# Second layer's projections of a four-layer graph network as three products of rounded halves and rests

## The chip, the cores and the metric

The kernel runs on one core of a Trainium2 chip. The metric is the device time of one execution in microseconds. The engines are TensorE (PE, matmuls), VectorE (DVE), ScalarE (ACT), GpSimd (POOL) and SyncE (SP, which here only issues transfers). Each engine works through its own instructions in the order in which they stand in the program, and semaphores order the engines against each other.

## What is computed

Four layers of a graph network, 1354 nodes with 256 features, one 1354x1354 adjacency matrix. Each layer is `x = x + layer(relu(layernorm(x)))`. The first layer (numbered 0 in the code) is an attention over all nodes. The change is in the second one (numbered 1):

```python
h  = relu(layernorm(x))
hW = h @ W_sa                                  # "h" items in the kernel
s_left, s_right = hW @ a_sa[0, :D], hW @ a_sa[0, D:]
e  = where(adj != 0, exp(-leaky_relu(s_left[:, None] + s_right[None, :], 0.01)), 0)
x_a = (e / (e.sum(1, keepdims=True) + 1e-5)) @ hW
x_b = adj @ (h @ W_gcnb) + b_gcnb              # "g" items in the kernel
attn_a = sigmoid(concat([adj @ h, h]) @ Wa.T + ba)
attn_b = sigmoid(concat([adj @ h, h]) @ Wb.T + bb)
x  = x + sigmoid(attn_a * x_a + attn_b * x_b)
```

The third and fourth layers are a neighbour mean with one projection and a masked attention.

## The kernel before, in words

The nodes are cut into NB = 11 blocks of up to 128 rows, and for the wide operands into NG = 3 groups of up to 512 columns. One n of NT = 33 "tiles" is a block of rows times a group. All data stays on the chip. Nearly every product of matrices is made exact enough in a cheap number format by splitting each operand into a rounded half and a rest (`hi` and `lo`, type float32r): ACT writes `hi`, DVE writes `lo = value - hi`, and PE adds three products, hi x hi, hi x lo, lo x hi (`products`, L333 to L337). The projections of the second layer are the exception: `project_full` (L1548 to L1551) multiplies plain float32 operands, two matmuls of 128x128 by 128x258 (or 260), each of which stands in the trace as two records.

The order of the work is written out by hand: each engine has a loop over steps `s`, and in step `s` it does a fixed list of things. Around the end of the first layer these are:

- PE, step s: `aggregate0(s-15)` (9 to 12 matmuls with the weights of tile s-15), and between them the second layer's first items: `turn(b, 1)`, which transposes normalised block b into PSUM bank 3 (one bank for all blocks, so `turn(b)` has to wait until block b-1 has been read out of it), `project_g(b)` and `project_h(b)`. Before: turn(0) in step 36, project_g(0) at the head of step 37, turn(1) to turn(3) at the ends of steps 37 to 39, project_g(1) to project_g(3) in steps 39 to 41, then turn(4) to turn(7) with the first project_h in steps 42 to 45. After the loop: project_h(4) to (7), and then the second layer's own aggregation `aggregate_b`, with turn(8) to turn(10) and the last projections between its tiles.
- ACT, step s: `exps(s-13)` (two exponentials), `z` (the normalised block), `h_full(b)` (L518: relu of the turned block into `h_mid`, plain float32), `g_hi` and `h1_hi` (rounded halves of the projections).
- DVE, step s: `weights_lo(s-14)` (L1004), `shift(s-12)` (L998), and in single steps more: `add_out(1)` in step 36 (L1012, L1016, four blocks of x), `stats` of three blocks in step 37 (L901), `stats`, four `aggr` and two small operations in step 38 (L901 to L911), `g_row_lo` in step 38 (L1028), `g_lo` from step 39 on (L1023). `weights_lo(n)` is what aggregate0(n) waits for before its last matmuls (L1642).
- POOL: `norm(1, 0)` and `norm(1, 1)` (L402, L409) turn the variances of the first eight blocks into scales; between them it has nothing to do.

The largest value of each column is found by `running` (L990), transposed by PE (`turn_max`, L1615), reduced on DVE (`top`, L958 to L966), spread again by PE (`spread_max`, L1624) and subtracted (`shift`). The last group's passes through this in steps 32 to 34.

`h_mid` lies in the memory of `mid_lo`, which the first layer's scores no longer need by then. The adjacency's rounded halves in the second layer (`adj_hi`, L684, on ACT; `adj_lo` on DVE, L1170, or POOL, L443) use the first columns of `mid_hi` and `mid_lo`.

Of the kernel before, what the change touches and what calls it, by code (L numbers as in the profile page):

```python
# [5 lines left out]
ALU = mybir.AluOpType  # L6
# [9 lines left out]
C = D // P  # L16
NB = -(-N // P)
# [21 lines left out]
def rows(b):  # L39
    return LAST if b == NB - 1 else P  # L40
# [64 lines left out]
def graph_layers_kernel(nc, x, adjT, wq, wk, wvT, wsa, wgcn, w2, w3, w3T, u3T, asa, cols, rws, eye, out):  # L105
    with ExitStack() as ctx:  # L106
# [3 lines left out]
        def sem(name):  # L110
            return ctx.enter_context(nc.semaphore(name))
# [64 lines left out]
        rb = sb("rb", [P, NB])  # L176

        hT0 = [t[:, 0:C * N].rearrange("p (c n) -> p c n", c=C) for t in (big_hi, big_lo)]
        hT3 = [t[:, :, :].rearrange("p b w -> p (b w)")[:, 0:C * N].rearrange("p (c n) -> p c n", c=C) for t in (v_hi, v_lo)]
        g = [t[:, :].rearrange("p (b w) -> p b w", w=W) for t in (big_hi, big_lo)]  # L180
        tT = [t[:, 0:C * N].rearrange("p (c n) -> p c n", c=C) for t in (mid_hi, mid_lo)]
# [74 lines left out]

        def h_block(b, layer):

            return [t[:, :, b * P:b * P + rows(b)] for t in (hT3 if layer == 3 else hT0)]

        ps = ctx.enter_context(nc.psum_tensor("ps", [P, 8, BANK], F32))
# [8 lines left out]
        def turns_before(layer):  # L270
            return NB * TURN_LAYERS.index(layer)
# [13 lines left out]
            sem(n) for n in ("col_set", "uw_set", "gram_set", "wlr_set", "wext_set"))  # L285
        whi, wlo = sems("whi", 7), sems("wlo", 7)
        st, mv, veps, rstd, ln = (sem(n) for n in ("st", "mv", "veps", "rstd", "ln"))
        zd, zt, hhi, hlo, h_set = (sem(n) for n in ("zd", "zt", "hhi", "hlo", "h_set"))
        x_add = sems("x_add", 4)
        t_mm, t_hi, t_lo = sems("t_mm", 2), sems("t_hi", 2), sems("t_lo", 2)  # L290
        v_mm, vhi, vlo = sems("v_mm", 2), sems("vhi", 2), sem("vlo")
# [22 lines left out]
        def wait(eng, s, value):  # L314

            if value > 0:
                eng.wait_ge(s, value)
# [7 lines left out]

        def h_done(eng, layer, count):

            if layer in (0, 3):
                wait(eng, hlo, (NB if layer else 0) + count)
            else:  # L330
                wait(eng, h_set, count)

        def products(eng, out_ap, lhs, rhs, first, last):  # L333

# [57 lines left out]
        def _(pool):  # L392
# [29 lines left out]
            pool.wait_ge(half_add, 1)  # L422
            for b in range(NB):
                add_bv(b)
            norm(1, 0)
            norm(1, 1)


# [73 lines left out]
        def _(act):  # L502
# [7 lines left out]
                act.activation(z_buf[:, b % 4, :], x_sb[:, b, :], ACT.Identity, bias=mr_all[:, b, 0:1],  # L510
                               scale=mr_all[:, b, 1:2]).then_inc(zd, 1)

            def h_full(b):

                act.wait_ge(zt, turns_before(1) + b + 1)
                if b == 0:
                    act.wait_ge(s_mm[0], NT)
                act.activation(h_mid[:, b, :, 0:rows(b)], turned(b, 1)[:, :, 0:rows(b)], ACT.Relu).then_inc(h_set, 1)  # L518

            def z2(b):  # L520

                act.wait_ge(ln, NG * 2 + b // PER + 1)
# [12 lines left out]
            def h_hi(b, layer):  # L535

                act.wait_ge(zt, turns_before(layer) + b + 1)
                act.activation(h_block(b, layer)[0], turned(b, layer)[:, :, 0:rows(b)], ACT.Relu).then_inc(hhi, 1)

            def t_hi_part(gi, a, parts=(0, 1)):  # L540
# [108 lines left out]
            for s in range(NB, NT + 13):  # L649
                if s >= 13:  # L650
                    exps(s - 13)
                if s == 11:
                    nonzero(1)
                    degree(1)
                elif 13 <= s < 31:
                    if s % 2:
                        nonzero((s - 13) // 2 + 2)
                    else:
                        degree((s - 13) // 2 + 2)
                if 33 <= s < 37:  # L660
                    z(s - 33, 1)
                if s == 35:
                    h_full(0)
                if 37 <= s < 40:
                    h_full(s - 36)
                if s == 37:
                    g_row_hi()
                if 38 <= s < 42:
                    g_hi(s - 38)
                if 39 <= s < 43:  # L670
                    z(s - 35, 1)
                if 42 <= s < 46:
                    h_full(s - 38)
                    h1_hi(s - 42)
                if 44 <= s < 46:
                    g_hi(s - 40)


            def adj_hi(n):

                wait(act, xb_mm, n - 2)
                if n == 0:
                    act.wait_ge(s_mm[0], NT)
                act.activation(adj_ring(at[0], n), adj_tile_b(n), ACT.Copy).then_inc(ahi, 1)  # L684

            def exp1(n):
# [51 lines left out]
            z(9, 1)  # L738
            z(10, 1)
            adj_hi(3)  # L740
            h_full(8)
            adj_hi(4)
            h_full(9)
            g_hi(8)
            h_full(10)
            exp1(0)
            g_hi(9)
            adj_hi(5)
# [137 lines left out]
        def _(dve):  # L886
# [26 lines left out]
            def h_lo(b, layer):  # L913

                hi, lo = h_block(b, layer)
                dve.wait_ge(hhi, (NB if layer else 0) + b + 1)
                dve.scalar_tensor_tensor(out=lo, in0=turned(b, layer)[:, :, 0:rows(b)], scalar=0.0, in1=f(hi), op0=ALU.max,
                                         op1=ALU.subtract).then_inc(hlo, 1)

# [194 lines left out]
            for s in range(NB, NT + LAG - 1):  # L1114
                if s == NB:
                    weights1_b()
                for gi in range(2):
                    if s == NB * gi + 12:
                        top(gi, 0, ALU.max)
                if s >= NT - 1:  # L1120
                    weights_lo(s - 14)
                if s == NT:
                    top(2, 0, ALU.max)
                for n in late_shifts(s):
                    shift(n, 0)
                if s < NT:
                    add(s)
                if s == 14:
                    weights_lo(0)
                if 13 <= s < NT - 1:  # L1130
                    shift(s - 13, 0)
                if 14 < s < NT - 1:
                    weights_lo(s - 14)
                for gi in range(2):
                    if s == NB * gi + 25:
                        add_out(gi)
                if s < NT:
                    running(s, 0, ALU.max)
                if s == 40:
                    dve.wait_ge(nz_sum, NB)  # L1140
                    dve.reciprocal(rdeg[:, :], deg[:, :]).then_inc(rdeg_set, 1)
                if 27 <= s < 31:
                    stats(s - 27, 1)
                if 27 < s <= 31:
                    aggr(s - 28, 1)
                if s == 37:
                    stats(4, 1)
                    stats(5, 1)
                    stats(6, 1)
                if s == 38:  # L1150
                    stats(7, 1)
                    for b in range(4, 8):
                        aggr(b, 1)
                if s == 38:
                    g_row_lo()
                if 39 <= s < 43:
                    g_lo(s - 39)
                if 43 <= s < 47:
                    h1_lo(s - 43)
                if 45 <= s < 47:  # L1160
                    g_lo(s - 41)
# [117 lines left out]
            adj_lo(2)  # L1279
            mask(1)  # L1280
            ramp(1)
            g_lo(8)
            adj_lo(4)
            g_lo(9)
            mask(2)
            ramp(2)
# [218 lines left out]
        def _(pe):  # L1505
# [39 lines left out]
                                   c == 0, c == C - 1)  # L1545
                return ins

            def project_full(out_ap, b, w, n):  # L1548

                for c in range(C):  # L1550
                    ins = pe.matmul(out_ap, h_mid[:, b, c, 0:rows(b)], w[:, c, 0:n], start=(c == 0), stop=(c == C - 1))  # L1551
                return ins

            def values(b, a):

                layer = 3 if a else 0
# [163 lines left out]
            def project_g(b):  # L1720

                h_done(pe, 1, b + 1)
                pe.wait_ge(wext_set, 2)
                pe.wait_ge(wg_in, 16)
                bank = item("g", b)
                project_full(ps[0:rows(b), bank, 0:W], b, raw_b, W).then_inc(g_mm, 1)

            def project_h(b):

                h_done(pe, 1, b + 1)  # L1730
                pe.wait_ge(wext_set, 1)
                pe.wait_ge(wsa_in, 16)
                bank = item("h", b)
                project_full(ps[0:rows(b), bank, 0:WA], b, raw_a, WA).then_inc(h_mm, 1)

            def lay_left(gi):

# [7 lines left out]
            for s in range(NB, NT + LAG):  # L1745
                if s < NT:
                    score(s, 0)
                if s == 36:
                    pe.wait_ge(s_sub[0], 2 * NB)
                    turn(0, 1)  # L1750
                if s == 37:
                    project_g(0)
                if s >= LAG:
                    aggregate0(s - LAG)
                for gi in range(NG):
                    if s == NB * gi + 11:
                        turn_max(gi, 0)
                    if s == NB * gi + 12:
                        spread_max(gi, 0)
                if 37 <= s < 40:  # L1760
                    turn(s - 36, 1)
                if 39 <= s < 42:
                    project_g(s - 38)
                if 42 <= s < 46:
                    turn(s - 38, 1)
                    project_h(s - 42)
                if 44 <= s < 48:
                    project_g(s - 40)
                if s == 46:
                    lay_left(0)  # L1770
# [261 lines left out]
```

## Time and profile before

| | |
|---|---|
| time before, median of 3 runs | 396.99 us (396.9 to 397.23) |
| profiled execution, its own time | 396.94 us |
| its span in the profile | 395.2 us |
| PE busy | 383.2 us (97%) |
| DVE busy | 336.9 us (85%) |
| ACT busy | 251.7 us (64%) |
| POOL busy | 121.9 us (31%) |
| mean granted clock of TensorE | 0.993 |

The second layer's first transposition starts at 103.8 us of the span, its last projection ends at about 151 us, and its aggregation runs up to about 240 us. A busy share of 97% on PE does not say that every us of PE work counts in full: in a stretch in which PE has no gap, time put on PE is time put on the kernel, and a stretch in which another engine is just ahead of PE has to be read separately. The PE records overlap in the trace, so the cost of a matmul is read from start to start, and not from its duration.

### The profile page before, as it was taken

The page shows a single profiled execution, that of the slowest core. Times are in us where ns is not written, and L with a number is a line of the kernel's source. Part 1 is how long each engine was busy: PE and PEld are TensorE (multiplying, and loading weights), DVE is VectorE, ACT ScalarE, POOL GpSimd, SP SyncE. Part 2 cuts the span into 40 slices and gives each one's busy share as a digit, 9 for nine tenths or more (in the row PEclk, how much of TensorE's full clock was granted, in tenths as well). Part 3 has the DMA queues.
Part 4 walks back from the last instruction along what each step waited for, and adds up shares of the span by engine and source line. Part 5 has one row for each costly group of instructions (what it writes and reads, how often), then busy time and mean ns, then how long its engine had stood idle before and what let it go on. Part 6 is the DMA issues. An engine that isn't in the chain of part 4 may idle for free. (4 is left out here: it accounts for less than half of the span.)

```text
span 395.2 us, 7759 instructions
## 1 busy us (share of the span) xinstructions
PE 383.2 (97%) x2647; PEld 354.4 (90%) x2647; DVE 336.9 (85%) x770; ACT 251.7 (64%) x531; POOL 121.9 (31%) x130
## 2 busy tenths in 40 slices
PE   8999999999999999999999999999999999989895
PEld 6888888999899899999999989998887898989894
DVE  5899899999984957999999989765887898799893
ACT  3553699888895658785787893245332576267772
POOL 1281000001010424223061011061010499379973
PEclk9999999999999999999999999999999999999988
DMA  7995000000000001000000000000000000010011
GB/s 233 375 380 189 0 2 1 2 0 2 0 2 0 2 1 55 2 2 0 3 2 0 3 0 2 2 1 0 2 2 0 2 1 2 0 55 1 2 54 37
DMA packets 10319, 13.99 MB, mean 35 GB/s; under 512 B 660, under 2 KB 7208, under 8 KB 10280
## 3 DMA queue, kind: packets, MB, share of 16 engines
q1 hardware_dynamic: 9736, 12.96, 9.6%
q10 hardware_dynamic: 544, 0.52, 0.4%
q8 instruction: 22, 0.36, 0.4%
q14 instruction: 17, 0.14, 0.1%
HBM read 12.10 MB, written 1.39 MB: 34 GB/s over the span
## 5 line engine op out<-in xcount | busy, mean ns | idle before, releaser
L1637 PE MATMUL ps<-v_hi,p_hi 128*128 128x258 f32 (+3 forms) x242 | 64.1, 295 | 0.3 <-DVE x_sb L1016 0.2
L402 POOL TENSOR_TENSOR mr_all<-mr_all,mhalf 128x4 f32<-128x4 f32 (+1 forms) x12 | 13.5, 1121 | 162.0 <-DVE mr_all L911 162.0
L1638 PE MATMUL ps<-v_lo,p_hi 128*128 128x258 f32 (+3 forms) x242 | 61.0, 282 | 0.0
L1637 PEld LDWEIGHTS ps<-v_hi,p_hi 128*128 128x128 f32 (+3 forms) x242 | 44.7, 185 | 2.1 <-issue 0.9
L1638 PEld LDWEIGHTS ps<-v_lo,p_hi 128*128 128x128 f32 (+3 forms) x242 | 44.8, 185 | 0.5
L1642 PE MATMUL ps<-v_hi,p_lo 128*128 128x258 f32 (+3 forms) x242 | 40.0, 283 | 1.1 <-DVE p_lo L1192 1.1
L998 DVE TENSOR_TENSOR s_sb<-s_sb,ps 128x512 f32<-128x512 f32 (+3 forms) x63 | 38.5, 612 | 1.3 <-PE ps L1624 1.2
L443 POOL TENSOR_TENSOR mid_lo<-adjT_sb,mid_hi 128x512 fp32r<-128x512 f32 (+2 forms) x16 | 22.5, 1406 | 48.5 <-ACT mid_hi L684 48.5
L1642 PEld LDWEIGHTS ps<-v_hi,p_lo 128*128 128x128 f32 (+3 forms) x242 | 32.5, 185 | 1.6 <-DVE p_lo L1192 1.6
L1928 PE MATMUL ps<-big_hi,p_lo 128*128 128x256 f32 (+3 forms) x121 | 32.2, 296 | 0.8 <-ACT p_lo L867 0.6
L1637 PE MATMUL ps<-big_hi,mid_hi 128*128 128x258 f32 (+3 forms) x121 | 31.8, 294 | 0.0
L1930 PE MATMUL ps<-big_lo,p_lo 128*128 128x256 f32 (+3 forms) x121 | 31.1, 287 | 0.0
L1638 PE MATMUL ps<-big_lo,mid_hi 128*128 128x258 f32 (+3 forms) x121 | 30.3, 282 | 0.0
L693 ACT ACTIVATE p_hi<-s_sb,minus_r 128x512 fp32r<-128x512 f32 (+3 forms) x33 | 22.1, 670 | 10.1 <-PE ps L1642 5.2
L1185 DVE SCALAR_TENSOR_TENSOR s_sb<-s_sb,sx 128x512 f32<-128x512 f32 (+3 forms) x33 | 26.0, 789 | 1.2
L990 DVE TENSOR_TENSOR m_sb<-m_sb,s_sb 128x512 f32<-128x512 f32 (+3 forms) x36 | 25.4, 704 | 0.7
L1928 PEld LDWEIGHTS ps<-big_hi,p_lo 128*128 128x128 f32 (+3 forms) x121 | 23.1, 191 | 2.5 <-ACT p_lo L867 2.1
L335 PE MATMUL ps<-mid_hi,v_hi 128*128 128x512 f32 (+3 forms) x66 | 25.2, 382 | 0.0
L335 PE MATMUL ps<-mid_hi,big_hi 128*128 128x512 f32 (+3 forms) x66 | 25.2, 381 | 0.0
L861 ACT ACTIVATE s_sb<-s_sb 128x512 f32<-128x512 f32 (+3 forms) x30 | 17.2, 574 | 11.4 <-DVE s_sb L998 11.3
L1426 DVE TENSOR_TENSOR w_lo<-ps,p_lo 128x512 fp32r<-128x512 f32 (+3 forms) x33 | 20.5, 620 | 4.7 <-ACT p_lo L867 3.2
L336 PE MATMUL ps<-mid_lo,big_hi 128*128 128x512 f32 (+3 forms) x66 | 24.3, 369 | 0.0
(249 smaller groups left out, 1217.9 us busy)
## 6 DMA issues: line engine op xcount, KB each, us to landing
adjT_sb<-in_adjT_dram SPq DMA_DIRECT2D x1, 2816.0 KB, 16.6
adjT_sb<-in_adjT_dram SPq DMA_DIRECT2D x3, 768.0 KB, 9.6
adjT_sb<-in_adjT_dram SPq DMA_DIRECT2D x1, 1815.0 KB, 21.5
out_dram<-x_sb SPq DMA_DIRECT2D x10, 128.0 KB
x_sb<-in_x_dram SPq DMA_DIRECT2D x2, 256.0 KB, 3.7
x_sb<-in_x_dram SPq DMA_DIRECT2D x1, 512.0 KB, 4.3
adjT_sb<-in_adjT_dram SPq DMA_DIRECT2D x1, 512.0 KB, 11.9
rows_sb<-in_rows_dram SPq DMA_DIRECT2D x1, 385.0 KB, 11.6
```

What stands on the lines that cost most here:

```text
L335: eng.matmul(out_ap, lhs[0], rhs[0], start=first, stop=False)
L336: eng.matmul(out_ap, lhs[0], rhs[1], start=False, stop=False)
L443: pool.tensor_tensor(adj_ring(at[1], n), adj_tile_b(n), f(adj_ring(at[0], n)), ALU.subtract).then_inc(alo_odd, 1)
L693: act.activation(ring(p_hi, n), sum1(n), ACT.Exp, bias=bias, scale=SLOPE - 1.0).then_inc(e_hi, 1)
L990: dve.tensor_tensor(m, m, mine(n), op).then_inc(s_max[a], 1)
L998: dve.tensor_tensor(mine(n), mine(n), ps[0:rows(j), bank, 0:CW[gi]], ALU.subtract).then_inc(s_sub[a], 1)
L1185: dve.scalar_tensor_tensor(out=sum1(n), in0=left[0:rows(j), gi, 0:CW[gi]], scalar=sx[0:rows(j), j, 0:1], in1=sum1(n), op0=ALU.add, op1=ALU ...
L1637: pe.matmul(out_ap, left_[0][0:k, n % RING, mine], right_[0][0:k, j, 0:cols_], start=(j == 0), stop=False)
L1638: pe.matmul(out_ap, left_[0][0:k, n % RING, mine], right_[1][0:k, j, 0:cols_], start=False, stop=False)
L1642: ins = pe.matmul(ps[0:rows(b), banks[b % PER], 0:cols_], left_[1][0:k, n % RING, mine], right_[0][0:k, j, 0:cols_], start=False, stop=(j ...
L1928: pe.matmul(sum3(b), p_lo[0:k, n % RING, mine], g[0][0:k, j, 0:D], start=(j == 0 and (gi == 2 or b % 2 == 0)), stop=False)
L1930: pe.matmul(sum3(b), p_lo[0:k, n % RING, mine], g[1][0:k, j, 0:D], start=False, stop=False)
```

## The change

Layer 1's turned blocks are now split as in the other layers: `h_hi` on ACT writes the half and a new `h_lo` on DVE the rest, 11 more DVE instructions. `project_full` goes; `project_g` and `project_h` call `project`, six float32r matmuls each. The weights are split too: ACT rounds `raw_b` in step 31 and `raw_a` in step 32, POOL subtracts both after `norm(1, 0)`. `project_g(0)` to `(3)` move from steps 37, 39, 40, 41 to steps 39 to 42, after the turn of their step. Since `h_done` now counts `hlo` in all layers, `turn(b, 1)` waits for `h_lo(b-1)` on DVE where it waited for `h_full(b-1)` on ACT. The waits of `adj_hi` change as well.

```diff
+        h1 = [t[:, :].rearrange("p (b c n) -> p b c n", b=NB, c=C) for t in (mid_lo, mid_hi)]
 ...
         def h_block(b, layer):
+            if layer == 1:
+                return [t[:, b, :, 0:rows(b)] for t in h1]
 ...
         def h_done(eng, layer, count):
-            if layer in (0, 3):
-                wait(eng, hlo, (NB if layer else 0) + count)
-            else:
-                wait(eng, h_set, count)
+            wait(eng, hlo, turns_before(layer) + count)
 ...   (POOL)
+            def weights_rest(k, lo, raw, hi):
+                pool.wait_ge(whi[k], 1)
+                pool.tensor_tensor(lo[:, :, :], raw[:, :, :], f(hi[:, :, :]), ALU.subtract).then_inc(wlo[k], 1)
             norm(1, 0)
+            weights_rest(4, wb_lo, raw_b, wb_hi)
+            weights_rest(3, wa_lo, raw_a, wa_hi)
             norm(1, 1)
 ...   (ACT; h_full goes, and each h_full(b) becomes h_hi(b, 1))
                 act.wait_ge(zt, turns_before(layer) + b + 1)
+                if layer == 1 and b == 0:
+                    act.wait_ge(s_mm[0], NT)
 ...
+                if s == 31:
+                    act.wait_ge(v_mm[0], NB)
+                    act.wait_ge(wg_in, 16)
+                    act.wait_ge(wext_set, 2)
+                    split(4, wb_hi[:, :, :], raw_b[:, :, :])
+                if s == 32:
+                    act.wait_ge(t_mm[0], 2 * NG)
+                    split(3, wa_hi[:, :, :], raw_a[:, :, :])
 ...
-                if 38 <= s < 42:
-                    g_hi(s - 38)
+                if 39 <= s < 43:
+                    g_hi(s - 39)
 ...
             def adj_hi(n):
-                if n == 0:
-                    act.wait_ge(s_mm[0], NT)
+                if n < RING:
+                    act.wait_ge(h_mm, 2 * n + 2)
 ...   (DVE)
+                if s == 36:
+                    h_lo(0, 1)
+                if 38 <= s < 41:
+                    h_lo(s - 37, 1)
                 if s == 38:
                     g_row_lo()
-                if 39 <= s < 43:
-                    g_lo(s - 39)
+                if 43 <= s < 47:
+                    h_lo(s - 39, 1)
+                if 40 <= s < 44:
+                    g_lo(s - 40)
 ...
             ramp(1)
+            h_lo(8, 1)
+            h_lo(9, 1)
             g_lo(8)
             adj_lo(4)
+            h_lo(10, 1)
             g_lo(9)
 ...   (PE)
-            def project_full(out_ap, b, w, n):
-                for c in range(C):
-                    ins = pe.matmul(out_ap, h_mid[:, b, c, 0:rows(b)], w[:, c, 0:n], start=(c == 0), stop=(c == C - 1))
-                return ins
 ...
-                pe.wait_ge(wext_set, 2)
-                pe.wait_ge(wg_in, 16)
+                pe.wait_ge(wlo[4], 1)
-                project_full(ps[0:rows(b), bank, 0:W], b, raw_b, W).then_inc(g_mm, 1)
+                project(ps[0:rows(b), bank, 0:W], b, 1, (wb_hi, wb_lo), W).then_inc(g_mm, 1)
 ...   (project_h likewise, with wlo[3], wa_hi, wa_lo)
-                if s == 37:
-                    project_g(0)
 ...
-                if 39 <= s < 42:
-                    project_g(s - 38)
+                if 39 <= s < 43:
+                    project_g(s - 39)
```

## Rows read from the trace of the kernel before

**Rows 1.** Busy time by stretch: us, then busy (instructions) of PE, PEld, DVE, ACT, POOL, clock
```profile
105.50:113.00 7.50, 7.50 (x53) 6.94 (x53) 7.37 (x25) 5.88 (x16) 1.44 (x2) 1.00 0.00 1
120.00:133.50 13.50, 13.50 (x84) 12.32 (x83) 7.38 (x22) 8.07 (x26) 0.78 (x3) 1.00 0.00 0
```
**Rows 2.** Timeline of PE, second layer's projections: start us, duration us, engine, line, operands
```profile
121.06 1.04 PE L1551 MATMUL ps<-raw_a,h_mid 128*128 128x260 f32 x4
121.94 1.03 PE L1551 MATMUL ps<-raw_b,h_mid 128*128 128x258 f32 x4
```
**Rows 3.** Timeline of PE: a first-layer projection in three products starts, the next work starts
```profile
29.79 0.28 PE L335 MATMUL ps<-wb_hi,big_hi 128*128 128x258 f32 x1
...
30.52 0.39 PE L335 MATMUL ps<-big_hi,wa_hi 128*128 128x512 f32 x1
```
**Rows 4.** Timeline of PE: project_g(0), then the starts of turn(1) and turn(2)
```profile
105.53 1.14 PE L1551 MATMUL ps<-raw_b,h_mid 128*128 128x258 f32 x4
...
107.84 0.38 PE L1512 MATMUL ps<-ident,z_buf 128*128 128x128 f32 x2
...
109.14 0.38 PE L1512 MATMUL ps<-ident,z_buf 128*128 128x128 f32 x2
```
**Rows 5.** Timeline of DVE, steps 37 to 39
```profile
107.43 0.49 DVE L1004 TENSOR_TENSOR p_lo<-s_sb,p_hi 128x330 fp32r<-128x330 f32 x1
...
111.06 0.42 DVE L1028 TENSOR_TENSOR big_lo<-rows_sb,big_hi 11x258 fp32r<-11x258 f32 x1
111.50 0.50 DVE L1004 TENSOR_TENSOR p_lo<-s_sb,p_hi 128x330 fp32r<-128x330 f32 x1
111.92 0.49 DVE L998 TENSOR_TENSOR s_sb<-s_sb,ps 128x330 f32<-128x330 f32 x1
```
**Rows 6.** DVE's groups by shape: the first layer's h_lo (count, busy us, mean ns)
```profile
L917 DVE SCALAR_TENSOR_TENSOR big_lo<-ps,big_hi 128x256 fp32r<-128x256 f32 x10 | 3.9, 413 | 0.0
```
**Rows 7.** Timeline of POOL: end of norm(1, 0), and a subtraction of 512 columns
```profile
98.96 0.20 POOL L409 TENSOR_TENSOR mr_all<-mr_all 128x4 f32<-128x4 f32 x1
...
139.04 1.09 POOL L443 TENSOR_TENSOR mid_lo<-adjT_sb,mid_hi 128x512 fp32r<-128x512 f32 x1 [1.26 <-ACT mid_hi L684]
```
**Rows 8.** Timeline of POOL (x_sb, 21.75 to 31.28) and of DVE's `running` beside and after it
```profile
21.75 9.53 POOL L415 TENSOR_TENSOR x_sb<-x_sb,rows_sb 128x256 f32<-128x256 f32 x11
...
29.42 1.25 DVE L990 TENSOR_TENSOR m_sb<-m_sb,s_sb 128x512 f32<-128x512 f32 x1
...
31.96 0.69 DVE L990 TENSOR_TENSOR m_sb<-m_sb,s_sb 128x512 f32<-128x512 f32 x1
```
**Rows 9.** Timeline of all engines, 98 to 102 us: the last column maxima, first layer
```profile
98.61 0.63 ACT L567 ACTIVATE p_hi<-s_sb 128x512 fp32r<-128x512 f32 x1 [1.42 <-DVE s_sb L998]
...
99.62 0.50 DVE L990 TENSOR_TENSOR m_sb<-m_sb,s_sb 74x330 f32<-74x330 f32 x1
...
100.17 0.55 PE L1615 MATMUL ps<-ident,m_sb 128*128 128x128 f32 x3 [0.61 <-DVE m_sb L990]
...
101.35 0.16 DVE L964 TENSOR_TENSOR mxr<-mxr,r_all 128x3 f32<-128x3 f32 x1
```
**Rows 10.** ACT and PE at turn(9): h_full(8), and the turn that waits for it
```profile
138.86 0.36 ACT L518 ACTIVATE h_mid<-ps 128x256 f32<-128x256 f32 x1
...
139.37 0.41 PE L1512 MATMUL ps<-ident,z_buf 128*128 128x128 f32 x2
```
**Rows 11.** PE's idle time in 226 to 229 us, clock unchanged
```profile
226.85 0.62 PE L1642 MATMUL ps<-v_hi,p_lo 128*128 128x258 f32 x3 [0.47 <-DVE p_lo L1192]
...
228.78 0.63 PE L1642 MATMUL ps<-v_hi,p_lo 128*128 128x258 f32 x3 [0.59 <-DVE p_lo L1192]
```
**Rows 12.** Busy time by stretch near the end: same columns as rows 1
```profile
371.00:372.00 1.00, 0.53 (x5) 0.32 (x3) 1.00 (x2) 0.77 (x2) 1.00 (x2) 1.00 0.00 0
...
373.00:374.00 1.00, 0.68 (x6) 0.55 (x5) 0.83 (x3) 0.88 (x3) 1.00 (x2) 1.00 0.00 0
...
375.70:379.10 3.40, 3.40 (x18) 3.40 (x18) 3.40 (x10) 2.79 (x7) 2.68 (x3) 0.50 0.06 22
```

More of the change, by code:

```diff
@@ L287, in graph_layers_kernel @@
         st, mv, veps, rstd, ln = (sem(n) for n in ("st", "mv", "veps", "rstd", "ln"))
-        zd, zt, hhi, hlo, h_set = (sem(n) for n in ("zd", "zt", "hhi", "hlo", "h_set"))
+        zd, zt, hhi, hlo = (sem(n) for n in ("zd", "zt", "hhi", "hlo"))
         x_add = sems("x_add", 4)
@@ L511, in z @@
                                scale=mr_all[:, b, 1:2]).then_inc(zd, 1)
-            def h_full(b):
-                act.wait_ge(zt, turns_before(1) + b + 1)
-                if b == 0:
-                    act.wait_ge(s_mm[0], NT)
-                act.activation(h_mid[:, b, :, 0:rows(b)], turned(b, 1)[:, :, 0:rows(b)], ACT.Relu).then_inc(h_set, 1)
             def z2(b):
@@ L662, in _ @@
                 if s == 35:
-                    h_full(0)
+                    h_hi(0, 1)
                 if 37 <= s < 40:
-                    h_full(s - 36)
+                    h_hi(s - 36, 1)
                 if s == 37:
                     g_row_hi()
-                if 38 <= s < 42:
-                    g_hi(s - 38)
+                if 39 <= s < 43:
+                    g_hi(s - 39)
                 if 39 <= s < 43:
@@ L672, in _ @@
                 if 42 <= s < 46:
-                    h_full(s - 38)
+                    h_hi(s - 38, 1)
                     h1_hi(s - 42)
@@ L681, in adj_hi @@
                 wait(act, xb_mm, n - 2)
-                if n == 0:
-                    act.wait_ge(s_mm[0], NT)
+                if n < RING:
+                    act.wait_ge(h_mm, 2 * n + 2)
                 act.activation(adj_ring(at[0], n), adj_tile_b(n), ACT.Copy).then_inc(ahi, 1)
@@ L740, in _ @@
             adj_hi(3)
-            h_full(8)
+            h_hi(8, 1)
             adj_hi(4)
-            h_full(9)
+            h_hi(9, 1)
             g_hi(8)
-            h_full(10)
+            h_hi(10, 1)
             exp1(0)
@@ L915, in h_lo @@
                 hi, lo = h_block(b, layer)
-                dve.wait_ge(hhi, (NB if layer else 0) + b + 1)
+                dve.wait_ge(hhi, turns_before(layer) + b + 1)
                 dve.scalar_tensor_tensor(out=lo, in0=turned(b, layer)[:, :, 0:rows(b)], scalar=0.0, in1=f(hi), op0=ALU.max,
@@ L1722, in project_g @@
                 h_done(pe, 1, b + 1)
-                pe.wait_ge(wext_set, 2)
-                pe.wait_ge(wg_in, 16)
+                pe.wait_ge(wlo[4], 1)
                 bank = item("g", b)
-                project_full(ps[0:rows(b), bank, 0:W], b, raw_b, W).then_inc(g_mm, 1)
+                project(ps[0:rows(b), bank, 0:W], b, 1, (wb_hi, wb_lo), W).then_inc(g_mm, 1)
             def project_h(b):
                 h_done(pe, 1, b + 1)
-                pe.wait_ge(wext_set, 1)
-                pe.wait_ge(wsa_in, 16)
+                pe.wait_ge(wlo[3], 1)
                 bank = item("h", b)
-                project_full(ps[0:rows(b), bank, 0:WA], b, raw_a, WA).then_inc(h_mm, 1)
+                project(ps[0:rows(b), bank, 0:WA], b, 1, (wa_hi, wa_lo), WA).then_inc(h_mm, 1)
             def lay_left(gi):
```

## The prediction

> **What bounds the kernel now.** I read first the busy time by stretch, around the end of the first layer. From 105.5 to 113 us PE is busy for all 7.50 of 7.50 us, and from 120 to 133.5 us again without a gap [rows 1]. So a us of PE work less is a us of kernel less there. The same rows carry the warning: in the first stretch DVE is busy for 7.37 of 7.50 us, in the second for 7.38 of 13.5. The change takes work from PE in both and puts work on DVE, and in the first DVE has no room. So I read next the timelines of PE and DVE over 97 to 120 us side by side, and then where POOL's new work would fall.
>
> **The gain on PE.** Two projections in a row start at 121.06 and 121.94 us [rows 2]: 0.88 us each. A first-layer projection of the same width in six float32r matmuls runs from 29.79 to 30.52 us: 0.73 us [rows 3]. There are 22 projections (11 g, 11 h): 22 x 0.15 = **3.3 us less**.
>
> **The new DVE work, and where it stands.** An h_lo takes 413 ns by its first-layer twin [rows 6]; back to back it adds about 0.34 us to the queue, since neighbours overlap by 0.08 (a weights_lo of 0.50 us is followed after 0.42 [rows 5]), and 0.41 until its result is there. From 120 us on DVE has room [rows 1], and nine of the eleven are hidden or nearly so. h_lo(0) and h_lo(1) are not, because of what `turn` now waits for. turn(2) needs h_lo(1). On DVE that stands in step 38, behind add_out(1), weights_lo(23), shift(25), three stats, weights_lo(24), shift(26), one stats, four aggr and two small ones, that is, exactly where g_row_lo stands before: 111.06 us [rows 5]. h_lo(0) ahead of it moves this by 0.34, and its own run takes 0.41: 111.81 us. Before, turn(2) started at 109.14 [rows 4]. So **turn(2) comes 2.7 us later**, whatever PE has saved by then, and everything that PE has behind it too. The wait falls in two parts: turn(1) already waits for h_lo(0), which stands behind add_out(1) (the next instruction starts at 107.43 [rows 5]) and ends at 107.84, while PE, without project_g(0) (0.88 us from 105.53 [rows 4]), reaches turn(1) at about 107.0.
>
> That 2.7 us does not yet hold project_g(0), which PE had done by then before and now has ahead of it: **+0.73 us**. Then turn(3) waits for h_lo(2), which follows g_row_lo, weights_lo(25) and shift(27) (0.44 + 0.42 + 0.42 [rows 5]) and takes 0.41: 1.7 us after h_lo(1), where PE needs 1.3 us from turn to turn [rows 4]: **+0.35** (0.4, less the last instruction's overlap). From turn(4) on, g_lo and h_lo keep up: between two turns PE has a tile and a projection of work, 1.1 + 0.73 us by [rows 3, 4], and in the stretch after, DVE was busy for only half of the time [rows 1].
>
> **The weights' split.** ACT idles for 1.42 us before exps(19) [rows 9]; the split of raw_b fits in, that of raw_a (about 0.6 us, as exps' own 512 columns take 0.63) delays exps(20), which has over 1 us in hand: nothing. The rests are on POOL, behind norm(1, 0), which ends at 99.16, each 516 or 520 columns, about 1.09 us [rows 7]: 99.2 to 100.3, and a second one behind it. At 99.62 DVE starts `running(32)`, whose result PE's turn_max is idle for (0.61 us, start 100.17 [rows 9]): the tightest place of this stretch. Both operands of `running` lie in SBUF, and the trace shows what that does beside POOL: during POOL's additions it takes 1.25 us, right after them 0.69 [rows 8]: 0.56 us more. If the second rest then lies over `top`'s two small additions (101.35 us [rows 9], also two SBUF operands), a further 0.0 to 1.1 us is at stake; I take that it starts after weights_lo(19), at 101.35, ends at 102.45 and holds the first of them until then. With the first delay of 0.6 to 0.7 the addition would be due at 102.0: 0.4 more. DVE's chain is then late by 1.1, and all of it comes back at turn(2), since DVE's queue has no gap of note on the way. Bounds: 0 (no hold, or POOL later than I think) and 2.2 (two full subtractions). I take **+1.1**.
> The Trainium skill's page SBUF — State Buffer, section "SBUF: two separate sides", says that a GpSimd instruction and a DVE instruction with two SBUF inputs exclude each other for a whole instruction, whichever started first. It speaks against this change. By it `running` would start only at POOL's end, 0.67 us late, where the row of 1.25 us gives 0.56; the sum would be 0.1 us higher.
>
> **Later waits.** turn(9) starts at 139.37, 0.15 us after h_full(8) ends (138.86 + 0.36) [rows 10]: it waited for it. Now h_lo(8) is in between, DVE being free: **+0.3**. And the four shorter project_h ahead of the second layer's first tile bring PE 0.6 us earlier to an adj_lo(0) that it already waited 0.2 us for, and DVE's queue ahead of that is shortened only in part: **+0.2**. adj_hi's new waits are for projections done long before: nothing.
>
> **The sum without the clock**: -3.3 + 2.7 + 0.73 + 0.35 + 1.1 + 0.3 + 0.2 - (project_g(0)'s 0.15 is in the 109.14 already, so only 21 savings count: +0.15) = **+2.2 us**.
>
> **The clock.** PE would stand still for about 1.2 us before turn(1) and 2.6 us before turn(2), with 1.2 us of work in between. The trace has two places with less. Idle times of 0.47 and 0.59 us within 2.4 us left the clock at 1.00 [rows 11]. Near the end, with PE busy 0.53 and 0.68 in two of three us (and eight matmuls of one column besides), it fell to 0.50, that is from 2.4 to 1.2 GHz, and stayed there from 375.7 to 379.1 us [rows 12]. Every us of PE work done so costs half a us. My idle time is above both, so I expect the fall, and a loss between 0 (it falls within the wait itself) and 2.6 us (it lasts twice as long, with the waits in it). I take **+1.5**, near the one stretch seen (half of 3.4, 1.7).
>
> Total: 396.94 + 2.2 + 1.5 = **400.6 us**. The profiled execution's 396.94 is 0.05 below the median, so nothing is added for that.
>
> **The rivals.**
> - *The waits, but no fall of the clock*, as at 226 us: +2.2, and with POOL's rests free as well +1.1: 398.0 to 399.2 us. For it: the rule of the fall is seen once only. Against: three times that idle time.
> - *The clock falls but POOL hinders nobody*: 396.94 + 1.1 + 1.5 = 399.5 us. For it: the first rest reaches the place only 0.4 us before `running` does (99.2 against 99.62), so a split or a norm that ends a little later puts it behind. Against: [rows 8], if it comes in time.
> - *More of everything*: both rests in DVE's way in full (2.2) and two stretches of slow clock: 396.94 + 3.3 + 2.6 = 402.8 us.
> - *The projections' gain comes through*: turn(2) finds h_lo(1) done. The place is DVE's step 38; it decides at whether h_lo(1) ends before PE reaches turn(2), at about 109.3. Then only the later waits remain: 396.94 - 3.3 + 0.5 = 394.1 us. Against it: the order of DVE's steps 36 to 38 has to be run through 1.8 us faster than it is now, with one instruction more. Only a misreading of the order would do it.
> - *Made good later*: PE waited 1.06 us for DVE at 226 to 229 [rows 11]; if DVE is not late with PE, up to 1.1 us comes back there; from the case without clock and POOL (+1.1) that ends at about 397.0 us, no change. Against: DVE's own start in the second layer hangs on PE's projections.
>
> **How the numbers follow.** Chances: the forecast 0.47, no fall of the clock 0.18, POOL hinders nobody 0.12, more of everything 0.11, made good 0.07, the gain comes through 0.05. Range: from 398.0 (the low end of the case without the clock) to 402.8. Slower by over 0.2% (0.8 us, about what a measurement of this kernel can tell from no change) are the first four, 0.88; within 0.2% is "made good", 0.07; faster is the last, 0.05.
>
> **What would show each step.** In the profile after: six matmuls per projection and starts 0.73 us apart; PE idle before turn(1) and before turn(2) at L1512, released by DVE's h_lo, 3 to 4 us in all; `running(32)` at about 1.2 us in place of 0.50 with POOL's subtraction beside it; granted clock 0.50 within some us behind turn(2). The prediction is wrong if turn(2) is not idle, which would say that I have DVE's order wrong; and too high by 1.5 if the clock stays at 1.00.

## The result and the profile after

The changed kernel takes 400.65 us (median of 4 runs, 399.49 to 400.89), against 396.99 before: ratio 1.0084, with an interval of 1.0070 to 1.0098. It is slower by 3.7 us. The profiled execution is the quickest of the four: 399.49 us, span 397.6, so 2.55 us over the profiled execution of before. That the other three are up to 1.4 us above it is part of the story.

The page's busy times, in the form of the table above:

```profile
span 397.6 us, 7847 instructions
...
PE 381.6 (96%) x2691; PEld 354.9 (89%) x2691; DVE 341.9 (86%) x781; ACT 253.3 (64%) x533; POOL 125.3 (32%) x132
```

PE is busy for 1.6 us less than before and the kernel is longer: the gain is there, and more than all of it went into waiting. Who PE waited for, in total, times, longest (us):

```profile
PE ps L1532 <- DVE mid_hi L928: 1.8, 3, 1.1
...
PE ps L1629 <- DVE m_sb L1001: 1.5, 2, 1.3
PE ps L1651 <- DVE x_sb L1027: 1.2, 2, 1.0
```

L1532 is `turn`, L928 `h_lo`, L1629 `turn_max` with `running` at L1001, and L1651 the first matmul of a tile, which waits for `add_out` at L1027. Before, the first wait was not there, the second was 0.8 us in all and the third 0.2 us. By stretch, in the columns of rows 1, the first line answers to its first line:

```profile
105.50:113.00 7.50, 5.35 (x31) 4.68 (x30) 7.25 (x25) 4.46 (x12) 0.77 (x1) 0.77 0.00 1
...
120.00:133.50 13.50, 13.50 (x116) 13.50 (x115) 8.58 (x22) 9.41 (x29) 0.47 (x2) 1.00 0.00 1
```

PE was busy for 7.50 of these 7.50 us; now 5.35, part of them at half clock, beside a DVE that is as full as before. In the second stretch it still has no gap: there the shorter projections pay nearly in full. The timelines of PE and DVE, with the idle time before an instruction and who ended it in brackets, answer to rows 4, 5 and 9:

```profile
98.92 1.30 POOL L429 TENSOR_TENSOR wb_lo<-raw_b,wb_hi 128x516 fp32r<-128x516 f32 x1
...
99.42 1.15 DVE L1001 TENSOR_TENSOR m_sb<-m_sb,s_sb 74x330 f32<-74x330 f32 x1
...
100.17 2.17 POOL L429 TENSOR_TENSOR wa_lo<-raw_a,wa_hi 128x520 fp32r<-128x520 f32 x1
...
100.63 0.55 PE L1629 MATMUL ps<-ident,m_sb 128*128 128x128 f32 x3 [1.27 <-DVE m_sb L1001]
...
101.81 0.56 DVE L975 TENSOR_TENSOR mxr<-mxr,r_all 128x3 f32<-128x3 f32 x1
...
107.28 0.36 PE L1651 MATMUL ps<-v_hi,p_hi 128*128 128x258 f32 x1 [1.02 <-DVE x_sb L1027]
...
108.92 0.63 PE L1532 MATMUL ps<-ident,z_buf 128*128 128x128 f32 x2
...
112.06 0.42 DVE L928 SCALAR_TENSOR_TENSOR mid_hi<-ps,mid_lo 128x256 fp32r<-128x256 f32 x1
...
112.62 0.41 PE L1532 MATMUL ps<-ident,z_buf 128*128 128x128 f32 x2 [1.13 <-DVE mid_hi L928]
...
114.35 0.41 PE L1532 MATMUL ps<-ident,z_buf 128*128 128x128 f32 x2 [0.24 <-DVE mid_hi L928]
```

The reader sees the chain of the prediction: beside POOL's first subtraction `running(32)` takes 1.15 us in place of 0.50, turn_max follows, beside the second one `top`'s first addition takes 0.56 in place of 0.16, and turn(2) starts at 112.62, when h_lo(1) (112.06 + 0.42) is done, 3.5 us later than in rows 4. At 107.28 stands a wait that the prediction did not have: aggregate0(22) waits for add_out(1). At turn(1) (108.92), where the prediction had a wait, there is none. And the projections, L335 to L337 in three products, follow each other 0.12 us apart from the second matmul on, as in rows 3.

### The profile page after: what moved, and what is told of

It reads as the page before. It is cut to its first block and busy times, and to the rows that moved or that the text cites. A ratio compares the mean times of both kernels' runs of the same rounds, so it can differ in the third digit from the quotient of the medians.

```text
span 397.6 us, 7847 instructions
## 1 busy us (share of the span) xinstructions
PE 381.6 (96%) x2691; PEld 354.9 (89%) x2691; DVE 341.9 (86%) x781; ACT 253.3 (64%) x533; POOL 125.3 (32%) x132
## 3 DMA queue, kind: packets, MB, share of 16 engines
HBM read 12.10 MB, written 1.39 MB: 34 GB/s over the span
## 5 line engine op out<-in xcount | busy, mean ns | idle before, releaser
L1651 PE MATMUL ps<-v_hi,p_hi 128*128 128x258 f32 (+3 forms) x242 | 63.3, 292 | 1.4 <-DVE x_sb L1027 1.2
L1651 PEld LDWEIGHTS ps<-v_hi,p_hi 128*128 128x128 f32 (+3 forms) x242 | 45.1, 186 | 3.0 <-ACT p_hi L570 1.2
L1651 PE MATMUL ps<-big_hi,mid_hi 128*128 128x258 f32 (+3 forms) x121 | 30.7, 285 | 0.0
L1001 DVE TENSOR_TENSOR m_sb<-m_sb,s_sb 128x512 f32<-128x512 f32 (+3 forms) x36 | 25.7, 715 | 0.7
L335 PE MATMUL ps<-mid_hi,v_hi 128*128 128x512 f32 (+3 forms) x66 | 25.2, 381 | 0.0
L335 PE MATMUL ps<-mid_hi,big_hi 128*128 128x512 f32 (+3 forms) x66 | 25.2, 381 | 0.0
```

The costliest lines, as they stand in the source:

```text
L335: eng.matmul(out_ap, lhs[0], rhs[0], start=first, stop=False)
L1001: dve.tensor_tensor(m, m, mine(n), op).then_inc(s_max[a], 1)
L1651: pe.matmul(out_ap, left_[0][0:k, n % RING, mine], right_[0][0:k, j, 0:cols_], start=(j == 0), stop=False)
```

## The experiments

### The changed kernel again, and its waits filled

The first question was the scatter, and whether the clock explains it. Beside a repetition, a kernel in which PE multiplies something during the waits:

```diff
+            def fill(count):
+                pe.wait_ge(s_add[0], NT)
+                pe.wait_ge(whi[4], 1)
+                for _ in range(count):
+                    pe.matmul(ps[:, 1, 0:W], wb_hi[:, 0, 0:P], wb_hi[:, 1, 0:W], start=True, stop=True)
 ...
+                if s == 37:
+                    fill(8)
                 if s >= LAG:
                     aggregate0(s - LAG)
+                if s == 38:
+                    fill(17)
```

> The changed kernel once more, unaltered, to have more executions of it beside those of the other kernels. Theory (the clock's fall costs an amount that depends on where it lies relative to the waits ahead of turn(1) and turn(2)): the times scatter by about 1.4 us (399.5 to 400.9 as so far) with an almost constant mean granted clock of 0.987 to 0.988. Rival (the 399.49 of the profiled execution was an outlier of another kind): all within 0.4 us of 400.7.

> The changed kernel with PE's waits filled: 8 more float32r matmuls of 258 columns (0.12 us each, 0.96 us) ahead of aggregate0(22), where PE idled 1.02 us, and 17 more (2.0 us) between aggregate0(23) and turn(2); they write a PSUM bank that nobody reads before it is written anew. Clock theory: PE no longer looks idle, the granted clock stays at 1.00 over 105 to 118 us, turn(2) starts when h_lo(1) is done as before (112.6), and the time is 399.2 to 399.6 in every execution, some 1.2 us under the changed kernel's median and with less scatter. Rival (the clock costs nothing here, or falls for another reason): 400.6 or, if the filling itself is in the way, up to 401.5.

Measured: the repetition 400.6 us (399.78 to 401.22, ratio 1.0082, 1.0069 to 1.0095), the filled one 399.84 (399.49 to 400.31, ratio 1.0068, 1.0056 to 1.0080). The repetition's profiled execution is its slowest, 401.22, and shows what the first one hid. First the repetition, then the filled kernel (busy time by stretch, same columns):

```profile
108.00:113.00 5.00, 2.65 (x21) 2.11 (x19) 4.93 (x19) 2.31 (x6) 0.41 (x1) 1.00 0.00 2
...
114.50:117.70 3.20, 3.18 (x16) 3.02 (x16) 1.97 (x6) 1.43 (x5) 0.00 (x0) 0.53 0.02 5
```

```profile
108.00:113.00 5.00, 4.67 (x38) 4.17 (x37) 4.93 (x19) 2.10 (x6) 0.62 (x1) 1.00 0.01 2
114.50:117.70 3.20, 3.20 (x27) 3.20 (x28) 2.10 (x6) 2.24 (x6) 0.00 (x0) 1.00 0.02 5
```

In the repetition PE idles for 2.35 of 5 us at full clock, and behind that runs from 114.5 to 117.7 at about half, 16 matmuls where the filled kernel does 27. turn(2) starts 13.2 us behind `running(32)` in both (112.99 and 112.77), so the filling neither helped nor hindered the wait itself. From turn(2) to the wait for adj_lo(0) in the second layer's first tile the repetition then takes 26.4 us and the filled kernel 25.1: the slow stretch costs 1.3 of the 1.55 us between the two executions. In the first profile the fall lay elsewhere:

```profile
108.10:111.45 3.35, 3.35 (x16) 2.98 (x16) 3.35 (x10) 1.86 (x5) 0.00 (x0) 0.52 0.01 2
```

There the slow stretch came before turn(2)'s wait: aggregate0(23) took longer, and PE then idled 1.13 us instead of 2.35. turn(2) is again 13.2 us behind `running(32)`, and 25.1 us follow to adj_lo(0): the slow clock was spent in time that PE had to wait anyway, which is 1.3 of the 1.7 us by which that execution is faster than the repetition's. So the fall is real, and in the one trace with filled waits it is absent; it costs 0 or 1.3 us according to where it lies. Between the two medians lie 0.8 us, though two of the repetition's five executions (399.78, 399.89) are among the filled kernel's times. What decides where it falls is not shown: idle times of 1.27 and 1.02 us were followed by it in the first profile, and of 1.27 and 1.06 us were not in the repetition. The expected median of 399.2 to 399.6 was a little missed (399.84), and so was "less scatter": 0.8 us remain, at mean granted clocks of 0.986 to 0.998; the kernel before scatters by 0.9 us at 0.985 to 0.998.

### POOL's subtractions: at another time, alone, and in the gaps

Three kernels. The first moves them to an earlier place (halves in steps 13 and 15, subtractions ahead of norm(1, 0)); the second adds nothing but the split to the kernel before; the third starts them right behind two `running`s:

```diff
+            pool.wait_ge(s_max[0], 27)
+            weights_rest(3, wa_lo, raw_a, wa_hi)
+            pool.wait_ge(s_max[0], 28)
+            weights_rest(4, wb_lo, raw_b, wb_hi)
             norm(1, 0)
-            weights_rest(4, wb_lo, raw_b, wb_hi)
-            weights_rest(3, wa_lo, raw_a, wa_hi)
 ...   (ACT: the halves in steps 23 and 25 instead of 31 and 32)
```

> The changed kernel with the weights split in steps 13 and 15 instead of 31 and 32, and POOL's two subtractions ahead of norm(1, 0), so that they lie near 45 us instead of 98.9 to 102.3 us. Theory (POOL's subtractions hold back running(32) and top's small addition, and DVE brings that lateness to turn(2)): running(32) takes 0.50 us again instead of 1.15, PE's idle time at L1629 is 0.6 instead of 1.27 us, h_lo(1) and turn(2) come 1.0 to 1.1 us earlier, and the median is 399.4 to 399.8. Rival 1 (the lateness is absorbed): unchanged, 400.4 to 400.8. Rival 2 (the subtractions hurt as much at 45 us): unchanged too, but with a running of about 1.2 us near 45 us and a PE wait there.

> The kernel before with only the weights' split added (ACT in steps 31 and 32, POOL behind norm(1, 0)); nothing reads the halves, the projections are plain float32. Theory (running(32) is held back by 0.65 us and top's first addition by 0.4, and PE waits for both): 0.8 us more than before, 397.7 to 398.0, with running(32) at 1.15 us. Rival (without the turn's wait for DVE, DVE's lateness does not reach PE beyond the 0.65 us at turn_max, or is made good): 397.0 to 397.5.

> The changed kernel with the weights' halves written in steps 23 and 25 and POOL's two subtractions started right behind running(29) and running(30), where DVE's next instructions (stats, add, shift, 1.3 us) have at most one operand in SBUF. Theory (a subtraction of 1.1 us on POOL costs only if a DVE instruction with two SBUF operands falls on it): no weights_lo or running in 90 to 100 us is longer than 0.70 us, PE's wait at L1629 is 0.6 us, turn(2) is 1.0 us earlier than in the changed kernel, median 399.4 to 399.8. Rival (any place in the first layer costs the same, since DVE or ACT is the bound there throughout, as with the subtractions at 52 and 58 us): 400.5 to 400.9.

Measured: earlier place 400.85 us (399.64 to 401.27), as rival 2 had it, though with the places near 52 and 58 us. The split alone 398.2 (398.03 to 398.44, ratio 1.0027, 1.0017 to 1.0037; the kernel before, measured beside it, 397.19): **+1.0 us**, a little over the 0.8 expected. In the gaps 399.69 (398.93 to 399.87, ratio 1.0061, 1.0048 to 1.0073): **0.9 us less** than the repetition (0.8 by the ratios), as expected. What the first did, on POOL, DVE and PE:

```profile
52.54 1.32 POOL L429 TENSOR_TENSOR wb_lo<-raw_b,wb_hi 128x516 fp32r<-128x516 f32 x1 [21.64 <-ACT wb_hi L512]
...
53.18 1.23 DVE L1001 TENSOR_TENSOR m_sb<-m_sb,s_sb 128x512 f32<-128x512 f32 x1
...
56.26 0.75 PE L1656 MATMUL ps<-v_hi,p_lo 128*128 128x258 f32 x4 [0.34 <-DVE p_lo L1015]
```

The same hold, 0.55 us, only in another step, and PE waits for DVE there instead; the second subtraction, at 57.70 us, holds a weights_lo for 0.95 us, and PE waits another 0.26. At neither place did DVE have slack. The kernel with the subtractions in the gaps has them beside instructions with at most one operand in SBUF:

```profile
93.96 0.49 DVE L1005 TENSOR_TENSOR m_sb<-m_sb,s_sb 128x330 f32<-128x330 f32 x1
...
94.53 1.31 POOL L429 TENSOR_TENSOR wb_lo<-raw_b,wb_hi 128x516 fp32r<-128x516 f32 x1 [1.09 <-DVE m_sb L1005]
...
95.17 0.68 DVE L1013 TENSOR_TENSOR s_sb<-s_sb,ps 128x512 f32<-128x512 f32 x1
...
96.37 0.50 DVE L1005 TENSOR_TENSOR m_sb<-m_sb,s_sb 128x330 f32<-128x330 f32 x1
```

No `running` is held, and turn_max starts at 100.02 us (before: 100.17). So it is neither POOL's work nor ACT's that costs, but the overlap with a DVE instruction that reads both operands from SBUF. The Trainium skill, SBUF — State Buffer, section "SBUF: two separate sides", says that these two exclude each other for a whole instruction. The trace agrees in kind, and in size about: in the changed kernel POOL's first subtraction starts at 98.92 and is recorded up to 100.22; `running(32)`, issued at 99.42, ends at 100.57, so that its own 0.50 us begin at 100.07. It is 0.65 us late, where the recorded end would give 0.80; the 0.67 and 0.56 of the prediction were for slightly other start times, so this case does not choose between them.

### project_g(0) one step later, alone

The kernel before, with project_g(0) to (3), g_hi and g_lo in the steps of the change and nothing else.

> The kernel before with only the order changed: project_g(0) to (3), g_hi and g_lo one step later, plain float32 projections, turn waits for ACT as before. Theory (project_g(0) covered the time until add_out(1) has emptied a bank for aggregate0(22)): PE idles 0.7 to 0.9 us ahead of aggregate0(22) and the kernel takes 0.8 us more, 397.7 to 397.9. Rival (PE works ahead and the wait is only moved): 396.9 to 397.2.

Measured: 398.08 us (397.85 to 398.33, ratio 1.0023, 1.0013 to 1.0033): **+0.9 us**, as the theory had it. On PE:

```profile
106.44 0.36 PE L1637 MATMUL ps<-v_hi,p_hi 128*128 128x258 f32 x1 [0.89 <-DVE x_sb L1016]
```

In the kernel before, project_g(0) (0.88 us) was what PE did while DVE emptied a PSUM bank for the last group of tiles. Taking it away left the hole.

### The turn's wait for DVE, alone

The kernel before with the 11 `h_lo` on DVE at the places of the change; they write a rest that nobody multiplies.

```diff
                 if turned_before(b, layer):
-                    h_done(pe, layer, turned_before(b, layer))
+                    wait(pe, hlo, turns_before(layer) + turned_before(b, layer))
 ...   (DVE)
+                if s == 36:
+                    h_lo(0, 1)
+                if 38 <= s < 41:
+                    h_lo(s - 37, 1)
 ...   (and 43 <= s < 47, and h_lo(8) to (10), as in the change)
```

> The kernel before (plain float32 projections, project_g(0) at the head of step 37, weights not split) with only DVE's part of the change: an h_lo per block at the places of the change, which writes a rest that nobody multiplies, and turn(b, 1) waiting for it. Theory (turn(2) waits for h_lo(1), which stands where g_row_lo stood): turn(2) at 111.8 to 112.0 instead of 109.14, turn(3) up to 0.35 us later still, turn(9) 0.3 us later: 3.2 to 3.4 us more than before without a fall of the clock (400.2 to 400.5), up to 402 with it. Rival (part of this wait is made good later, as PE waits for DVE near 226 us anyway): 398.5 to 399.5.

Measured: 401.9 us (401.14 to 402.5), ratio 1.0110 (1.0094 to 1.0125), the kernel before beside it 397.25: **+4.65 us**, the largest part by far.

```profile
107.94 0.41 PE L1527 MATMUL ps<-ident,z_buf 128*128 128x128 f32 x2
111.77 0.41 PE L1527 MATMUL ps<-ident,z_buf 128*128 128x128 f32 x2 [2.36 <-DVE mid_hi L918]
```

turn(2) at 111.77 in place of 109.14 is 2.6 us, where rows 4 to 6 gave 2.7. By the same trace turn(3) adds 0.45 us and turn(9) 0.45, and the clock, which fell behind this wait too (mean 0.87 over 105 to 118 us), 1.4. This trace is of the slowest of the four executions (402.5 us), so the 4.65 us probably hold less of the clock's price than that.

### h_lo(1) ahead, and a new order

Is it h_lo(1) alone? The changed kernel with h_lo(1) right behind weights_lo(24):

> The changed kernel with h_lo(1) on DVE directly behind weights_lo(24) instead of behind shift(26), a stats, four aggr and two small ones. Theory (turn(2) waits for h_lo(1) and for nothing else): turn(2) 1.2 to 1.3 us earlier relative to the start of add_out(1), PE's wait there nearly gone at half clock, the rest of the step as before, median 399.2 to 399.8. Rival (exps or weights_lo of the next steps become late instead, since shift(26) comes 0.34 us later): 400.2 to 400.8.

Measured: 399.79 us (399.7 to 402.58, ratio 1.0079, 1.0056 to 1.0102). The median would suit the theory, but the timeline does not:

```profile
112.03 0.41 PE L1534 MATMUL ps<-ident,z_buf 128*128 128x128 f32 x2 [1.47 <-DVE mid_hi L928]
...
114.65 0.66 PE L1534 MATMUL ps<-ident,z_buf 128*128 128x128 f32 x2 [1.14 <-DVE mid_hi L928]
```

turn(2) comes 1.0 us earlier than in the repetition, and turn(3) at 114.65 where it was at 114.72: h_lo(2), which still stood behind DVE's variances, took over. Nothing of note was won up to turn(3); with a scatter from 399.7 to 402.6 the median says little. The queue had to be reordered as a whole: h_lo(0) ahead of add_out(1), h_lo(1) and (2) behind their step's shift, stats and aggr spread over three steps, project_g(0) back at the head of step 37, together with POOL's subtractions in the gaps.

```diff
+                if s == 36:
+                    h_lo(0, 1)
+                if s in (37, 38):
+                    h_lo(s - 36, 1)
                 for gi in range(2):
                     if s == NB * gi + 25:
                         add_out(gi)
 ...
-                if s == 37:
-                    stats(4, 1)
-                    stats(5, 1)
-                    stats(6, 1)
-                if s == 38:
-                    stats(7, 1)
+                if s in (37, 38):
+                    stats(s - 33, 1)
+                if s == 39:
+                    stats(6, 1)
+                    stats(7, 1)
                     for b in range(4, 8):
                         aggr(b, 1)
```

> The changed kernel with the subtractions as in the one behind running(29) and (30), and a new order: h_lo(0) ahead of add_out(1), h_lo(1) and h_lo(2) right behind shift(25) and shift(26), the four stats and aggr spread over steps 37 to 39, g_row in steps 41 and 42, z(4) to z(7) one step later, project_g(0) back at the head of step 37 and (1) to (3) in 39 to 41. Theory (the three products' gain of 3.2 us is real and only DVE's order around steps 36 to 38 ate it): PE waits 0.3 to 0.6 us for h_lo(0), under 0.5 us in all at turn(1) to turn(3), the clock stays up, and the median is 393.9 to 395.0, faster than both. Rival (DVE's extra 3.8 us of h_lo has to be paid in this stretch whatever the order): 396.5 to 398.

Measured: 396.2 us (396.07 to 396.91), ratio 0.9981 (0.9972 to 0.9990): faster than both, and below the rival's 396.5 to 398, but 1.2 us short of what was expected. Two waits remained in its trace:

```profile
105.79 0.39 PE L335 MATMUL ps<-wb_hi,mid_lo 128*128 128x258 f32 x1 [0.49 <-DVE mid_hi L932]
...
119.33 0.41 PE L1537 MATMUL ps<-ident,z_buf 128*128 128x128 f32 x2 [0.67 <-DVE mid_hi L932]
```

A further order takes h_hi ahead of z on ACT, g_row later, h_lo(0) ahead of shift(24), h_hi(8) ahead of adj_hi(3):

> The kernel with the subtractions behind running(29) and (30) and the new order, further: h_lo(0) ahead of shift(24), h_hi(4) to (7) ahead of z on ACT, g_row in step 45 on ACT and 46 on DVE, h_hi(8) ahead of adj_hi(3). Theory (what that kernel still lost were PE's waits of 0.49 us ahead of project_g(0), 0.67 us at turn(5), where h_hi(4) stood behind z and g_row on ACT, and 0.45 us at turn(9)): project_g(0)'s wait 0.1 us, none at turn(5), 0.1 to 0.3 at turn(9), and 1.0 to 1.3 us less than its 396.2: 394.9 to 395.2. Rival (the next thing in the queue takes over): 395.6 to 396.2.

Measured: **395.65 us** (395.33 to 396.17), ratio 0.9961 (0.9948 to 0.9973): 1.6 us faster than the kernel before. It is 0.55 us less than 396.2 (0.8 by the ratios), not the 1.0 to 1.3 expected: this is the rival's range. The waits at turn(5) and turn(9) are gone; that ahead of project_g(0) stayed, as h_lo(0) now waits for ACT's h_hi(0):

```profile
105.47 0.42 DVE L933 SCALAR_TENSOR_TENSOR mid_hi<-ps,mid_lo 128x256 fp32r<-128x256 f32 x1 [0.25 <-ACT mid_lo L543]
...
105.95 0.39 PE L335 MATMUL ps<-wb_hi,mid_lo 128*128 128x258 f32 x1 [0.42 <-DVE mid_hi L933]
```

### The gain of the three products, in that order

The same kernel, with the two projections as plain float32 matmuls on the rounded half.

> The kernel of better order with the projections back to two plain float32 matmuls each, on the rounded half of the block and the unsplit weights; the rests are still made and waited for, but not multiplied, so the projections leave out the rests' part. Theory (a plain projection takes 0.88 us of PE, three products 0.73, and PE is the bound wherever the 22 stand): 3.0 to 3.3 us more than the kernel of better order. Rival (part of the shorter projections is only waited away): 1.5 to 2.5 us more.

Measured: 398.86 us (397.7 to 399.24), 3.2 us more than the kernel of better order. But 1.05 us of three of these five executions lie outside the profiled span: time and span differ there by 2.94 to 2.96 us, and by 1.7 to 2.1 us in all other executions of these kernels; what it is, is not shown. By the spans alone, median 396.2 against 393.8, the plain projections cost **2.4 us more**, which is the rival's range of 1.5 to 2.5. The traces say the same: from project_g(0) to the waits at 225.13 (better order) and 227.47 us (plain) the difference grows by 2.5 us. Of the 22 x 0.15 = 3.3 us the first is lost whole. First the tile behind project_g(0) in the kernel of better order (project_g(0) at 105.95, above), then project_g(0) and that tile with plain projections:

```profile
107.06 0.36 PE L1657 MATMUL ps<-v_hi,p_hi 128*128 128x258 f32 x1
```

```profile
105.79 1.14 PE L1577 MATMUL ps<-raw_b,mid_lo 128*128 128x258 f32 x4 [0.41 <-DVE mid_hi L933]
106.90 0.36 PE L1663 MATMUL ps<-v_hi,p_hi 128*128 128x258 f32 x1
```

Both take 1.11 us from project_g(0) to the start of aggregate0(22), which is the tile that waits for add_out(1). Up to turn(5) five projections save 0.34 us in place of 0.75, the next eleven 1.39 in place of 1.65, the last six 0.77 in place of 0.90.

## Why the prediction was right, and where not

The forecast of 400.6 us met the median of 400.65, and slower was right, by the mechanism that was named. That the total is so near is luck: the sum without the clock was +2.2 us, and the kernel with filled waits is 2.8 us slower than the kernel before; the clock was +1.5, and is 0.8. Two errors of 0.6 and 0.7 us cancel. Step by step:

- **The gain on PE**, 3.3 us: oversized. Between the last two kernels it is 2.4 to 2.5 us. In the changed kernel's profile, from turn(3) to the waits of rows 11, the time is 1.66 us shorter than before, with project_g(0) (0.73) added and turn(9) 0.3 later: 2.7 us for the 21 savings that the sum counts as 3.15. Rows 2 and 3 are projections in a stretch without any wait; near the turns part of the saving is waited away.
- **turn(2) waits for h_lo(1)**, 2.7 us later: 2.6 with that wait alone, 3.5 in the changed kernel together with POOL's part (3.8 by the sum). Right, and the main cause: alone it and its followers, with the clock's fall behind it, cost 4.65 us.
- **project_g(0)'s place.** The time was counted (0.73 us), the reason for a loss was not seen whole. The prediction put a wait of 1.2 us ahead of turn(1); it stands one tile earlier, 1.02 us ahead of aggregate0(22), for add_out(1). I had asked what turn waits for, and not what the moved projection had covered. Moved alone it costs 0.9 us. In the sum this changed nothing, since turn(2)'s wait begins after it and swallows it; in a kernel without that wait it would have been an error of 0.9 us.
- **turn(3)**, 0.35 us: PE idles 0.24 us, and turn(3) is 0.45 us later still than turn(2). **turn(9)**, 0.3 us more: it idled 0.45 us, for h_lo(8), where it had waited 0.15. Right.
- **The adj_lo(0) at the second layer's first tile**, 0.2 us: wrong. PE idles 0.20 us there as it did before (0.21).
- **POOL's subtractions**, 1.1 us: turn_max 0.66 us and h_lo's queue about 1.05 us late in the first profile, +1.0 alone, -0.9 without. Right, with both of its two places: `running(32)` 0.65 us late, `top`'s first addition 0.40.
- **The clock**, 1.5 us: oversized. The fall came, but between the medians it costs 0.8 us (0 in the profiled execution, 1.3 in the slowest of the repetition). What was wrong is taking the full price of one slow stretch in every execution: in some it falls into a wait.

The parts measured alone: 1.0 (split) + 0.9 (order of g) + 4.65 (turn's wait, clock included) - 2.4 (by the spans) = 4.15 us, against 3.66 for the whole. The parts need not add up, since the waits share time and the clock's price differs; the 0.5 us between were not traced further. The rival "made good later" fell: PE's waits near 229 to 231 us in the changed kernel are 0.48 and 0.61 us, the 0.47 and 0.59 of rows 11, only shifted. The rival "the gain comes through" had -2.8 us against the kernel before; with a new order of DVE, ACT and PE and POOL's subtractions in the gaps, -1.0 and -1.6 us of it were reached. In the faster one turn(3) is still 0.9 us later than in the kernel before, and 1.7 us of lead stand at the waits of rows 11.

## What to carry to other kernels

Shortening PE's work pays only where the other queue has room: before a producer's step is added to an engine's queue, read what stands ahead of it in that queue, and compare this with the time at which the consumer arrives. When an instruction group is moved, ask also what it covered at its old place. Small work on POOL cost nothing here when it started behind a DVE instruction with two SBUF operands and 1.2 us passed to the next such one; beside one it cost 1.0 us. Time a change by the spans as well as by the medians: here they differ by 0.8 us in one comparison.

## What the runs showed of the hardware

The same kernel with the same mean granted clock of 0.988 took 399.49, 399.78, 400.6, 400.68, 400.87 and 400.89 us, and at 0.993 once 401.22: the mean clock does not give the price. In the traces of 399.49 and 401.22 us a stretch of 3.2 to 3.35 us at about half clock cost nothing where PE would have waited for DVE, and 1.3 us behind the wait; where it lay in the others is not shown. So a wait of 2 us on PE should be priced with and without it. A trace of the quickest execution, as the first one here, hides that price. And a POOL subtraction of 516 or 520 columns beside a DVE instruction with two SBUF operands held that instruction by 0.40 to 0.95 us in four places, while instructions with one SBUF operand kept their length beside it (0.68 us at 95.17).
